# One graph-attention layer on one core: the register load behind a comparison, the first node tile in three pieces

## The reference

```
HW = x @ W;  s = HW @ a[:512];  t = HW @ a[512:]
e  = leaky_relu(s[row] + t[col], 0.2)           # per edge
att = softmax of e over the edges of a row
agg = segment_sum(att * x[col], row)
out = silu(agg) @ base_w.T + einsum(basis(agg), spline_w)   # 8 cubic B-splines
result = layernorm(x + out)
```

## Time and profile before

| | |
|---|---|
| three runs | 387.41, 388.95, 388.98 us (median 388.95) |
| the profiled execution | 386.36 us, span of its instructions 384.6 us |
| TensorE busy | 370.0 us, 96% of the span |
| VectorE / ScalarE / GpSimd busy | 336.8 / 253.6 / 37.1 us |
| granted TensorE clock | 0.998 of full speed |
| chain that ended last, by engine | TensorE 86%, VectorE 8%, ScalarE 2% |

### The profile page before, as it was taken

One profiled execution on the slowest core, in us unless ns is written; L12 is line 12 of the kernel. 1 busy time (PEld: TensorE's weight loads), 2 busy tenths in 40 slices (PEclk: granted clock), 3 DMA queues, 4 the chain that ended last, 5 costly groups with the idle time before them and its releaser, 6 DMA issues.

```text
span 384.6 us, 5446 instructions
## 1 busy us (share of the span) xinstructions
PE 370.0 (96%) x2082; PEld 304.6 (79%) x2082; DVE 336.8 (88%) x428; ACT 253.6 (66%) x252; POOL 37.1 (10%) x92
## 2 busy tenths in 40 slices
PE   7797899999999999999999999999999999999994
PEld 3676568888888888888888888888888888888883
DVE  8998799987764889999899997988999799999455
ACT  6769745445337979874876874896766696766122
POOL 6001301000000010101001010100100101010000
PEclk9999999999999999999999999999999999999999
DMA  7911987000000066577644546342343353453102
GB/s 253 399 23 40 221 147 217 2 2 0 2 0 0 2 208 179 168 239 219 179 151 149 180 119 203 117 109 56 114 128 88 104 146 109 154 192 111 55 27 109
DMA packets 23979, 47.28 MB, mean 123 GB/s; under 512 B 1936, under 2 KB 2412, under 8 KB 23954
## 3 DMA queue, kind: packets, MB, share of 16 engines
q0 software_dynamic: 12416, 24.00, 23.7%
q1 hardware_dynamic: 11538, 22.95, 18.4%
HBM read 44.37 MB, written 2.57 MB: 122 GB/s over the span
## 4 chain that ended last, share of the span: by engine, by line
PE 86%; DVE 8%; ACT 2%; issue 2%; POOL 1%; DVEq 1%; POOLq 0%
PE PS L1414 38%; PE PS L1410 25%; PE PS L1351 18%; PE PS L1333 3%; DVE oh L557 2%; DVE still L573 2%; PE PS L1361 1%; ACT C L1045 1%; DVE hit L536 1%; DVE oh L523 1%; ACT Z L1050 1%; PE PS L1424 0%; ACT xl L1055 0%; DVE pat L546 0%; DVEq L301 0%
## 5 line engine op out<-in xcount | busy, mean ns | idle before, releaser
L1414 PE MATMUL PS<-wh,s 128*128 128x512 f32 x432 | 139.4, 390 | 0.0
L1414 PEld LDWEIGHTS PS<-wh,s 128*128 128x128 f32 x432 | 81.2, 188 | 16.8
L1410 PE MATMUL PS<-s,wh 128*128 128x482 f32 x288 | 92.8, 383 | 0.0
L1414 PE MATMUL PS<-wl,s 128*128 128x512 f32 x216 | 84.2, 390 | 0.0
L1144 ACT ACTIVATE s<-v 128x1220 fp32r<-128x1220 f32 (+1 forms) x32 | 40.0, 1251 | 37.5 <-DVE v L932 26.3
L1410 PEld LDWEIGHTS PS<-s,wh 128*128 128x128 f32 x288 | 54.6, 189 | 9.7
L1127 ACT ACTIVATE v<-xt,bias 128x1220 f32<-128x1220 f32 (+1 forms) x32 | 42.9, 1341 | 20.1 <-DVE s L942 18.1
L1410 PE MATMUL PS<-s,wl 128*128 128x482 f32 x144 | 55.2, 384 | 0.0
L926 DVE SCALAR_TENSOR_TENSOR v<-v,v 128x1220 f32<-128x1220 f32 (+1 forms) x32 | 46.4, 1451 | 6.3 <-ACT v L1130 6.3
L932 DVE SCALAR_TENSOR_TENSOR v<-v,v 128x1220 f32<-128x1220 f32 (+1 forms) x32 | 46.8, 1461 | 3.3
L514 POOL DMA_DIRECT2D wh<-in_splT x32 | 23.0, 718 | 256.1 <-PE PS L1414 183.0
(11 more groups left out here) (162 smaller groups left out, 427.3 us busy)
## 6 DMA issues: line engine op xcount, KB each, us to landing
wh<-in_splT POOLq DMA_DIRECT2D x32, 512.0 KB, 4.2
wring<-in_splT SPq DMA_DIRECT2D x21, 512.0 KB, 4.5
xt<-in_xT SPq DMA_DIRECT2D x1, 2500.0 KB, 12.2
xh<-in_x POOLq DMA_DIRECT2D x1, 2304.0 KB, 11.8
wh<-in_baseT POOLq DMA_DIRECT2D x4, 512.0 KB, 5.5
out<-xr SPq DMA_DIRECT2D x8, 256.0 KB
wring<-in_baseT SPq DMA_DIRECT2D x3, 512.0 KB, 4.0
xr<-in_x SPq DMA_DIRECT2D x1, 1280.0 KB, 5.9
```

Source lines behind the costliest of these rows:

```text
L1410: m = e.matmul(PS[:, w, 0:TURNED], wx[:, ic, 128 * w:128 * w + 128], sx[:, ic, 0:TURNED], start=begins, stop=ends_)
L1414: m = e.matmul(PS[:, out_bank(w), :], sx[:, ic, c:c + 128], wx[:, ic, :], start=begins, stop=ends_)
```

## The change

1. The register load moves from group 8 to group 9 on VectorE and TensorE (`LOADS_AT`), and `left_table` from behind group 8's comparison to behind group 9's `hits`.
2. `minus_x` stands at batches 7 to 16 instead of 11 to 17 and behind the loop; `st_rows` on TensorE at groups 3 to 6 instead of 4 to 7, on ScalarE at batch 11 instead of 13; `s_part` ahead of batch 17's casts.
3. Tile 0 has three pieces, 0:256, 256:768, 768:1250. In PSUM and in `ph` its blocks are rotated by eight places, so that `pl` is still made in two pieces, blocks 2 to 5 and then 6 to 9, 0 and 1. The first part of tile 1's `bent` is 180 columns instead of 500 and stands behind the first `weigh`.
4. The marks of the last 250 columns for tiles 2 to 9 are made by ScalarE behind the second exponential.
5. ScalarE's fifth exponential stands behind the fourth tile's `p_high`.

```diff
-HALF, NEXT, BEGUN = 512, 880, 500
+HALF, NEXT, BEGUN = 512, 880, 180
+FIRST_ROWS = (0, 256, 768, N)
-        LOADS_AT = 8
-        NEGATIVE_AT = {11 + k: k for k in range(NT - 3)}
+        LOADS_AT = 9
+        NEGATIVE_AT = {7 + k: k for k in range(NT)}
         def pieces(j):
-            return ((0, HALF), (HALF, N)) if j == 0 else ((0, N),)
+            return tuple(zip(FIRST_ROWS, FIRST_ROWS[1:])) if j == 0 else ((0, N),)
         def place(j, k):
-            return (k + 2 * (j % 2)) % NT
+            return (k + (2 * (j % 2) if j else NT - 2)) % NT
...
@@ VectorE
+                if g == 9:
+                    left_table()
                 one_hot_still(g)
...
-                if g == 8:
-                    left_table()
...
+                e.tensor_tensor(den0[:, 3:4], den0[:, 1:2], den0[:, 2:3], ALU.add).then_inc(s_two, 1)
+                e.wait_ge(s_two, 1)
...
             bent(0, NEXT, N).then_inc(s_z, 1)
+            weigh(0, 0)
             bent(1, 0, BEGUN).then_inc(s_begun, 1)
-            weigh(0, 0)
             weigh(0, 1)
+            weigh(0, 2)
             greatest(1)
...
             weigh(1)
-            marks(MARKED, ND, NEAR, NT).then_inc(s_marked, 1)
             e.wait_ge(s_marked, 1)
             greatest(2)
...
             inverse(2)
+            e.wait_ge(s_marked, 2)
             greatest(3)
@@ ScalarE
-                if b == 13:
+                if b == 11:
                     st_rows()
+                if b == 17:
+                    ...
                 for w, n in TAKEN:
...
-                if b == 17:
-                    ...
-            for k in range(len(NEGATIVE_AT), NT):
-                minus_x(k)
...
+            def last_marks(j0, j1):
+                d = slice(DW * MARKED, N)
+                e.wait_ge(s_p, 1)
+                e.activation(Z[:, j0:j1, d], C[:, j0:j1, d], ACT.Relu, bias=bias[:, 2 * NP + 1:2 * NP + 2], scale=-BIG
+                             ).then_inc(s_marked, 1)
             grow(0, 0)
             grow(0, 1)
+            grow(0, 2)
             p_high(0, 0)
             p_high(0, 1)
+            p_high(0, 2)
             grow(1)
+            last_marks(NEAR, NEAR + 1)
+            last_marks(NEAR + 1, NT)
             p_high(1)
...
+                if j == 2:
+                    grow(4)
...
-                if j + 3 < NT:
+                if 1 < j < NT - 3:
                     grow(j + 3)
@@ TensorE
-                if g in (4, 5, 6, 7):
-                    st_rows(g - 4)
+                if g in (3, 4, 5, 6):
+                    st_rows(g - 3)
...
             turn(0, 1)
             sums(0, 0, 0)
+            turn(0, 2)
             sums(0, 0, 1)
+            sums(0, 0, 2)
             sums(0, 2, 0)
+            sums(0, 2, 1)
             sums(0, 1, 0)
+            turn(1)
             sums(0, 1, 1)
-            turn(1)
-            sums(0, 2, 1)
```

More of the change, by code:

```diff
@@ L168, in build @@
         den = sb("den", [128, 2, NT])
-        den0 = sb("den0", [128, 2])
+        den0 = sb("den0", [128, 4])
         st = sb("st", [128, 5, 6])
@@ L249, in build @@
         s_setup = sem("s_setup")
-        (s_reach, s_bits, s_col, s_mk, s_bound, s_left, s_tab, s_mi, s_ln, s_table, s_hit, s_mv, s_head, s_ovk, s_ovm, s_ovs, s_ova, s_ovz, s_marked, s_early, s_near, s_touch, s_first, s_next, s_begun, s_late, s_tmax, s_small, s_z, s_p, s_den, s_rden, s_plo,
+        (s_reach, s_bits, s_col, s_mk, s_bound, s_left, s_tab, s_mi, s_ln, s_table, s_hit, s_mv, s_head, s_ovk, s_ovm, s_ovs, s_ova, s_ovz, s_marked, s_early, s_near, s_touch, s_first, s_next, s_begun, s_late, s_tmax, s_small, s_z, s_p, s_two, s_den, s_rden, s_plo,
          s_a3, s_b3, s_spl, s_slo, s_wlo, s_res, s_bns, s_bna, s_rstd, s_nb, s_fin) = (
             sem(f"v_{n}") for n in (
-                "reach", "bits", "col", "mk", "bound", "left", "tab", "mi", "ln", "table", "hit", "mv", "head", "ovk", "ovm", "ovs", "ova", "ovz", "marked", "early", "near", "touch", "first", "next", "begun", "late", "tmax", "small", "z", "p", "den", "rden", "plo",
+                "reach", "bits", "col", "mk", "bound", "left", "tab", "mi", "ln", "table", "hit", "mv", "head", "ovk", "ovm", "ovs", "ova", "ovz", "marked", "early", "near", "touch", "first", "next", "begun", "late", "tmax", "small", "z", "p", "two", "den", "rden", "plo",
                 "a3", "b3", "spl", "slo", "wlo", "res", "bns", "bna", "rstd", "nb", "fin"))
@@ L306, in pieces, with blocks, upto_low, blocks_added @@
         def pieces(j):
-            return ((0, HALF), (HALF, N)) if j == 0 else ((0, N),)
+            return tuple(zip(FIRST_ROWS, FIRST_ROWS[1:])) if j == 0 else ((0, N),)
         def upto(j, p=0):
+            return p + 1 if j == 0 else j + 3
+        def blocks(j, p):
+            return ((0, 2), (2, 6), (6, NT))[p] if j == 0 else (0, NT)
+        def upto_low(j, p=0):
             return p + 1 if j == 0 else j + 2
-        def blocks(j, p):
-            return ((0, 4), (4, NT))[p] if j == 0 else (0, NT)
+        def blocks_added(j, p):
+            return ((0, ADDED[1]), (ADDED[1], NT))[p] if j == 0 else (0, NT)
+        def blocks_low(j, p):
+            return ((2, 6), (6, NT + 2))[p] if j == 0 else (0, NT)
+        def places(j, a, b):
+            return (place(j, a), place(j, a) + b - a) if j == 0 else (a, b)
         def smalls(j):
@@ L852, in inverse @@
                 d = den[:, 0, j:j + 1]
-                e.wait_ge(s_p, j + 2)
+                e.wait_ge(s_p, upto(j, len(pieces(j)) - 1))
                 if j == 0:
-                    e.tensor_scalar(d, den0[:, 0:1], den0[:, 1:2], 1e-30, ALU.add, ALU.max).then_inc(s_den, 1)
+                    e.tensor_tensor(den0[:, 3:4], den0[:, 1:2], den0[:, 2:3], ALU.add).then_inc(s_two, 1)
+                    e.wait_ge(s_two, 1)
+                    e.tensor_scalar(d, den0[:, 0:1], den0[:, 3:4], 1e-30, ALU.add, ALU.max).then_inc(s_den, 1)
                 else:
@@ L861, in p_low @@
             def p_low(j, p=0):
-                a, b = blocks(j, p)
-                e.wait_ge(s_phi, upto(j, p))
+                a, b = places(j, *blocks_low(j, p))
+                e.wait_ge(s_phi, upto(j, p + 1) if j == 0 else upto(j))
                 if j >= 3:
@@ L1061, in _ @@
                            PS[:, 6:8, 0:4].rearrange("p b (a c) -> p a b c", c=2)).then_inc(s_wa, 1)
-                if b == 13:
+                if b == 11:
                     st_rows()
+                if b == 17:
+                    e.wait_ge(s_sc, 4)
+                    for k, (lo, hi) in enumerate(TCH):
+                        e.mul(s_part[:, lo // 128:hi // 128],
+                              PS[:, 6 + k % 2, lo // 64:hi // 64].rearrange("p (j a) -> p j a", a=2)[:, :, 0], SLOPE - 1
+                              ).then_inc(s_scol, 1)
                 for w, n in TAKEN:
@@ L1090, in p_high @@
             def p_high(j, p=0):
-                a, b = blocks(j, p)
+                a, b = places(j, *blocks(j, p))
                 e.wait_ge(s_t, upto(j, p))
@@ L1327, in turn @@
                 if j >= 2:
-                    e.wait_ge(s_plo, upto(j - 2, len(pieces(j - 2)) - 1))
+                    e.wait_ge(s_plo, j)
                 for k in range(a, b):
                     if j and k == 8:
-                        e.wait_ge(s_plo, upto(j - 1, len(pieces(j - 1)) - 1))
+                        e.wait_ge(s_plo, j + 1)
                     q = place(j, k)
@@ L1339, in sums @@
                 pp, xs = ((ph, xh), (pl, xh), (ph, xl))[i]
-                end = 2
-                a, b = blocks(j, p)
+                end = 2 if j else 1
+                a, b = (blocks, blocks_low, blocks_added)[i](j, p)
                 if j >= 2 and i == 0:
@@ L1347, in sums @@
                     e.wait_ge(s_xa[p], (16, 48)[p])
-                if i < 2:
-                    e.wait_ge((s_phi, s_plo)[i], upto(j, p))
+                if i == 0:
+                    e.wait_ge(s_phi, upto(j, p))
+                if i == 1:
+                    e.wait_ge(s_plo, upto_low(j, p))
                 for t in range(a, b):
-                    m = e.matmul(PS[:, 5 + j % 2, :], pp[:, j % 3, place(j, t), :], xs[:, t, :],
-                                 start=(i == 0 and t == 0), stop=(i == end and t == NT - 1))
-                if i == end and b == NT:
+                    m = e.matmul(PS[:, 5 + j % 2, :], pp[:, j % 3, place(j, t), :], xs[:, t % NT, :],
+                                 start=(i == 0 and t == 0), stop=(i == end and t == b - 1 >= NT - 1))
+                if i == end and b >= NT:
                     m.then_inc(s_agg, 1)
```

9 lines of the change are left out of this document (2 added, 7 removed).

## The result

| | before | after |
|---|---|---|
| median of 20 runs each | 387.19 us | 388.93 us |
| the profiled execution | 386.36 us | 388.39 us |
| span of its instructions | 384.6 us | 386.6 us |
| TensorE granted clock over the span | 0.998 | 0.992 |
| second node tile's products begin | 59.50 us | 61.49 us |

The ratio is 1.0042, 95% interval 1.0029 to 1.0055: **slower by 0.4%**, where I forecast 0.5% faster. The three runs before the prediction (median 388.95) lay high; over 20 runs the kernel before takes 387.19, so by its own step of minus 2.0 us the forecast would read 385.2. Against that the changed kernel is 3.7 us late: what failed is a step of the working, not the scale.

The account below looks back on a forecast made before the run. Bound: TensorE, full from the second tile's products at 59.50 us, whose start ScalarE's idle times delay. Minus 1.57 for those and 0.43 for the pieces gives 2.0 us: 388.95 to 386.9, range 385.2 to 388.8.

Parts of the forecast that it names:

- What bounds the kernel: TensorE is full from the second node tile's products at 59.50 us, so the end moves only with their start.
- The load: VectorE's and TensorE's register loads move behind ninth-group work; VectorE's 1.41 us, beside a comparison, was costed at 0.1 us.
- Minus x and the rows on ScalarE: ScalarE loses two idle times before its last counts casts: minus 1.57 us, counts ending at 42.4.
- Row transfers: Rows of s and t ready at 29.2 instead of 32.5; broadcasts at unchanged lengths land at 37.7 and 40.2, in time.
- Rival (b): Row transfers queue behind x's transfers, the second broadcast lands at 44.8, 2.3 us late: 389.2 us; chance 0.08.
- Three pieces: First tile in three pieces: second transposes at 48.2, 0.64 us beyond the shift, less 0.22 for more transposes; net about 0.4.
- x late for its correction: Rival: first tile's xl products wanted at 52.3, x lands at 50.5; each us past 52.3 costs one; chance 0.07.
- Last marks on ScalarE: Takes 0.68 us off VectorE, adds two activations of 1.75 us (bounds 1.5 and 2.5) on ScalarE, hidden.
- Fifth exponential: On ScalarE, moved behind the fourth tile's cast; worth 0 either way, as TensorE is full there.

Follow-up runs that it names:

- rows_written_first: The changed kernel with the first accumulating transfer of x held until the four writes of t_row have landed; 384.95 us, 0.9953 to the kernel before.
- load_alone: The kernel before with only the register load moved (group 9, left_table behind its hits); 385.74 us, ratio 0.9976.
- x_just_before: rows_first_swapped with x's first transfer permitted at the fifth minus-x, behind the t_row writes and just ahead of the broadcasts; 385.03 us, ratio 0.9949.
- load_back: The changed kernel with the register load and left_table back at their old places (group 8); 390.12 us, ratio 1.0088.
- rows_first_swapped: rows_written_first with TensorE's xl products of the first tile's last six blocks exchanged with its first four pl products; 384.22 us, ratio 0.9925.
- series_changed: The changed kernel with fourteen one-value register loads on SP from 31.4 us, the t_row writes behind them; VectorE's load 4849 ns, no kernel time given.
- load_late: rows_first_swapped with both register loads at the twelfth and last group; 384.38 us, ratio 0.9933.
- the probes: The changed kernel and rows_first_swapped, each with eight five-value register loads added on SP behind gentle's issue; loads 1.05 to 3.57 us, no kernel times given.

## Why the prediction was wrong

*What bounds the kernel*: right. In every profile the span moved with the start of the second tile's products: 324.9 to 325.1 us lie from there to the end.

*The load*: the step "I cost it at 0.1 us", with "the cover is worth nothing", failed. Its price came from a row taken while the queues were nearly empty (2 GB/s over 30 to 36 us); the same change put a 1 MB accumulating transfer beside it. It cost 2.16 us on VectorE; TensorE stood 1.84 us ahead of its tenth group (0.36 in rows_written_first), and then its granted clock fell: 0.71, 0.50, 0.50 and 0.58 of full speed in the four microseconds from 39. Over 35.90 to 44.00 us it was 0.79 (columns as in the earlier trace rows, where it was 1.00):

```profile
35.90:44.00 8.10, 6.22 (x93) 5.74 (x89) 5.88 (x12) 6.16 (x13) 2.31 (x3) 0.79 1.07 231
```

So the group began 1.4 us later than in rows_written_first, and its 74 matmuls took 5.25 us at a granted clock of 0.67 instead of 3.72 at 1.00: half of what the long load cost TensorE came with the lower clock. With the queues empty the step holds: load_alone hides it whole.

*Minus x and the rows on ScalarE*: right up to 40.0 us; with x held the whole step holds: VectorE's third block of the first tile starts at 46.18 in rows_written_first, where I had 46.07 and the earlier trace rows 47.64.

*Row transfers*: **this is the step that decided**: "With the same lengths they land at 37.7 and 40.2 ... they need no more than stay equal". Ready sooner they were (SP at 29.22, as forecast), but the lengths went from 3.5, 5.0 and 7.1 us to 7.6, 8.0 and 9.4. Rival (b) had the mechanism and the consequence: it priced the second landing at 44.8 and the kernel at 389.2; they came at 46.6 and 388.9. That 389.2 lies so near is luck: it stood on a base of 388.95, 1.8 us high, and meant a loss of 0.3 us where 1.7 were measured. Its rate was luck too: of what moved from 36 to 44 us before, at the 204 GB/s of the earlier trace rows, 1.30 of 1.64 MB were the broadcasts' own; x alone happens to move as fast, but was through at 41.5 and not at 38.6, since its packets came in full number only from 32 us on (11 in 31 to 32 us, 93 in the next). I gave (b) 0.08, and what I held against it failed. "Today's broadcasts already share with one such transfer" was read from issue times that overlap; by the queues' packets the broadcasts went first and x met only `gentle`'s last 2 us, and the list of issues could have told: x's first part took 13.0 us to land in the kernel before, and 8.9 in the changed one where it came first, so it was x that stood behind. (Even behind them it cost them something: they take 4.0 and 5.2 us alone, 5.0 and 7.1 in the kernel before.) That the broadcasts would get a turn while x moved was my estimate: in 38 to 40 us x moved 196 packets and the waiting broadcast none. Some sharing there is: 146 packets of x and 55 of the rows in 40 to 42 us here, 116 and 54 in 38 to 40 in x_just_before.

How the two causes share the loss is read from the timelines and was not run apart: the counts' end at 44.65 is about 2.2 us later than with x held, the rows hold VectorE's first full block to 46.72 against 42.71, 4.0 us. The rows were the later of the two, and the load's cost lay beneath them. Where the load was uncovered (load_back) it became the bound.

*Three pieces*: with x held, the steps came as forecast (second batch of transposes at 48.33, I had 48.2); of the 0.43 net, x took all but 0.14 in rows_written_first, and it was reached when x's products stood behind four others. By its own terms the last step was 9.2 us (9.09 less 0.1 plus 0.22) and not 9.3; rows_first_swapped took 9.1, from 48.22 to 57.33. The runs give 0.6 us for the third cut and the two edits with it; the cut by itself wasn't run.

*x late for its correction*: the size I left it, landing at 50.5, held in the changed kernel (40.87 plus 9.1 is 50.0), where nothing waited for it. Once the rows go first it is late by 0.36 us, and by 2.27 if held until they land.

*Last marks on ScalarE*: 2.13 us for both, hidden as forecast. *Fifth exponential*: TensorE is full from 61.5 to 133.4 us, so 0.

## What to carry to other kernels

An edit on one engine that frees a permission earlier starts a transfer earlier (x at 28.74 instead of 35.70 us here): ask what small, urgent transfer is issued after it, and let the big one wait for that. Read who had the queues from packets by stretch, not from overlapping issue times, and take a wait's price only from a moment with the same traffic. Hold the big transfer no longer than until the small ones are issued: waiting for their landing cost 3.8 us.

## What the runs showed of the hardware

- A register load of one value took 0.25 us on SP and 0.47 on TensorE; in series_changed mostly 1.0 to 1.8 us on SP until about two thirds of x's first and of its second part had moved (0.72 of 1.05 MB by 35.7 us, 0.50 of 0.79 by 40.4). Five values took 1.41 us on VectorE, and 4.5 to 4.9 beside such a transfer. A plain copy at 395 GB/s beside it changed nothing (1.42). What in the accumulating transfer does it, why mostly in its first part, and why load_late (1.44 and 0.52) and most loads of the probes (1.05 to 1.65) escaped, is open.
- x's first two parts, whose issues had ended 6.7 and 0.7 us before that of `trow` began (30.09 and 36.10 against 36.81), moved nearly whole ahead of the broadcasts: 8.0 and 9.4 us for those, which take 4.0 and 5.2 alone. With x's issue ended between theirs (x_just_before) the later one shared and took 9.6.
- One of SP's own issues was longer in that time: 0.99 us for `gentle` where it had been 0.42.
- The accumulating transfer moved about 205 GB/s, the same one as plain copy up to 395.
